# Two transformer blocks on one core: block 1's softmax is divided after its attention matmul, and GpSimd does block 0's clamped normalising

## What is computed

```
x  = x + attn0(ln(x)) + experts0(ln(x))     # block 0
x  = x + attn1(ln(x)) + ffn1(ln(x))         # block 1

attn0: 16 heads of 16 channels, causal, scores + slope * (k - q)
       attn = maximum(softmax(scores), 1e-10);  attended = attn @ v;  attended @ out_w.T + out_b
attn1: 16 heads of 16 channels, causal
       y = softmax(q @ k.T * scale) @ v;  y @ Wo + bo
```

## Time and profile before

| | us |
|---|---|
| median of 3 runs (lowest, highest) | 873.58 (872.56, 874.31) |
| span of the profiled execution | 874.1 |
| PE busy, DVE busy, ACT busy, POOL busy in it | 689.0, 676.7, 589.6, 179.4 |
| one steady pass (430.8 to 524.5) | 93.7 |
| first pass and setup (0 to 147) | 147 |
| last pass (712.5 to 819.8), final stage (819.8 to 874.1) | 107.3, 54.3 |

### The profile page before, as it was taken

The page is one execution under the profiler, slowest core; times in us unless marked ns, Lnnn a source line. Parts: engine busy times, 40 slices in busy tenths (PEclk is TensorE's granted clock), DMA queues, the critical chain, the costliest instruction groups (busy, mean ns, idle before and its releaser), DMA issues.

```text
span 874.1 us, 19430 instructions
## 1 busy us (share of the span) xinstructions
PE 689.0 (79%) x5824; PEld 538.0 (62%) x5824; DVE 676.7 (77%) x2591; ACT 589.6 (67%) x1753; POOL 179.4 (21%) x205
## 2 busy tenths in 40 slices
PE   0676645889869996989788987899789968897756
PEld 0454434667647775767676775677577756685523
DVE  3978755879877996798688987799679986897485
ACT  2455421787759784888488775978497838966764
POOL 6011021132112212131113211321113111320221
PEclk9889876999989998999989998999899998898965
DMA  6752005040323114030504041312312050300651
GB/s 195 257 144 85 1 1 156 1 145 15 107 64 102 43 57 126 24 121 12 170 1 144 13 132 39 109 36 85 98 66 79 13 156 2 128 18 1 198 187 49
DMA packets 55196, 73.95 MB, mean 85 GB/s; under 512 B 4544, under 2 KB 47680, under 8 KB 55104
## 3 DMA queue, kind: packets, MB, share of 16 engines
q1 hardware_dynamic: 52064, 69.22, 25.9%
q0 software_dynamic: 1056, 2.62, 1.0%
q10 hardware_dynamic: 1984, 1.21, 0.4%
HBM read 42.10 MB, written 30.93 MB: 84 GB/s over the span
## 4 chain that ended last, share of the span: by engine, by line
DVE 31%; PE 26%; issue 18%; ACT 16%; DMA 5%; ACTq 1%; SPq 1%; DVEq 1%; POOL 1%; POOLq 0%
DVE probs L1291 7%; DVE probs L1303 7%; PE gen_ps L948 6%; ACT probs L852 4%; PE gen_ps L991 3%; PE gen_ps L959 3%; PE value_ps L1032 3%; PE gen_ps L979 3%; ACT hid L839 3%; DVE acc L1251 2%; DVE gated L1236 2%; ACT pt L861 2%; PE turn_ps L1009 2%; PE gen_ps L934 1%; DMA gu_lo<-x_dram 1%
## 5 line engine op out<-in xcount | busy, mean ns | idle before, releaser
L852 ACT ACTIVATE probs<-probs,nmax 128x256 f32<-128x256 f32 (+1 forms) x512 | 227.5, 447 | 84.9 <-DVE nmax L1291 84.1
L1291 DVE CUSTOM_DVE_ANT_0 probs<-score_ps,bias 128x256 f32<-128x256 f32 (+1 forms) x512 | 159.9, 350 | 49.5 <-PE score_ps L1003 46.9
L1303 DVE TENSOR_SCALAR probs<-probs,rsum 128x256 f32<-128x256 f32 (+1 forms) x512 | 180.4, 394 | 9.1
L724 POOL TENSOR_TENSOR h_lo<-hid,h_hi 128x512 f16<-128x512 f32 x64 | 76.6, 1197 | 424.5 <-ACT h_hi L832 409.4
L861 ACT ACTIVATE pt<-turn_ps 128x384 f32<-128x384 f32 x256 | 122.1, 477 | 33.2 <-PE turn_ps L1011 33.2
L948 PE MATMUL gen_ps<-xe_hi,gu_hi 128*128 128x256 f16 x512 | 104.4, 288 | 4.6 <-DVE v_sb L1162 4.1
L1009 PE MATMUL turn_ps<-ident,probs 128*128 128x128 f32 x256 | 78.1, 305 | 34.0 <-DVE probs L1303 29.1
L948 PE MATMUL gen_ps<-xe_lo,gu_hi 128*128 128x256 f16 x512 | 104.1, 287 | 0.0
L948 PE MATMUL gen_ps<-xe_hi,gu_lo 128*128 128x256 f16 x512 | 103.4, 286 | 0.0
L852 ACT ACTIVATION_READ_ACCUMULATOR probs<-probs,nmax 128x1 f32 x512 | 97.4, 190 | 0.0
L1002 PE MATMUL score_ps<-k_stack,q_stack 96*128 96x256 bf16 x256 | 73.7, 292 | 24.3 <-DMA k_stack<-scr_k 16.0
(11 more groups left out here) (164 smaller groups left out, 1511.4 us busy)
## 6 DMA issues: line engine op xcount, KB each, us to landing
q_stack<-scr_q SPq DMA_DIRECT2D x32, 384.0 KB, 3.8
k_stack<-scr_k SPq DMA_DIRECT2D x32, 384.0 KB, 5.2
scr_q<-parts SPq DMA_DIRECT2D x16, 384.0 KB, 2.6
scr_k<-parts SPq DMA_DIRECT2D x16, 384.0 KB, 3.3
scr_q<-parts SPq DMA_DIRECT2D x16, 256.0 KB, 3.6
scr_k<-parts SPq DMA_DIRECT2D x16, 256.0 KB, 3.6
x<-in_x SPq DMA_DIRECT2D x8, 256.0 KB, 3.6
scr_q<-parts SPq DMA_DIRECT2D x16, 128.0 KB, 2.9
```

Source lines behind the costliest of these rows:

```text
L724: pool.tensor_tensor(h0_lo[:, e], hid0[:, e], h0_hi[:, e], ALU.subtract).then_inc(s_h0l, 1)
L852: last = act.activation(probs[:, k, lo:hi], probs[:, k, lo:hi], ACT.Exp, scale=-1.0, bias=nmax[:, k, j:j + 1], accum_out=esum[:, k, j:j + 1])
L1291: last = dve.tensor_tensor_reduce(out=probs[:, k, lo:hi], in0=g[:, lo:hi], in1=bias[:, blo:S], scale=-1.0, scalar=BIG, op0=ALU.add, op1=AL ...
L1303: last = dve.tensor_scalar(probs[:, k, lo:hi], probs[:, k, lo:hi], rsum[:, k, j:j + 1], *clamp)
```

## The change

Block 1: the exponentials stay as they are. PE's `turn` waits for the exponential itself (`s_ex`) in place of `s_nm`. ACT puts the row sums in `esum1`, ordered by unit. After each unit DVE takes one reciprocal of them, spread over 16 channels ([128 x 256], L1342 of the new file). PE transposes that in two fp32 matmuls into the free half of the `value_ps` bank (L1071), ACT copies it to `rows1` in place of copying the values, and DVE multiplies values and `rows1` into `at` (L1350).

Block 0: DVE still takes the reciprocal of each head. The two multiply-and-clamp instructions move to POOL's queue (L756), at the place of `norm` in the list.

```
+                if name == "norm" and head_block(st) == 0:          # POOL's queue
+                    k = st.arg % PROBS
+                    wait(pool, s_rz, clamped_before(st, 1))
+                    if st.kind == "steady":
+                        settle(pool, s_gps)
+                    for lo, hi, j in ((0, S, 0), (S, S + P, 1)):
+                        last = pool.tensor_scalar(probs[:, k, lo:hi], probs[:, k, lo:hi], rsum[:, k, j:j + 1], CLAMP,
+                                                  ALU.mult, ALU.max)
+                    last.then_inc(s_nm, 1)
...
+                if name == "value" and st.arg % 2 == 1 and set_block(st) == 1:   # ACT's queue
+
+                    wait(act, s_pv, sets_before(st, 1))
+                    act.activation(rows1[:].rearrange("p t q -> p (t q)"), value_ps[:, S:2 * S], ACT.Copy).then_inc(s_rw, 1)
...
-                    wait(pe, s_nm, heads_before(st, 1))
+                    wait(pe, *((s_nm, clamped_before(st, 1)) if head_block(st) == 0 else (s_ex, heads_before(st, 1))))
...
+                    if l == 1 and r == 1:                            # PE's queue, end of a unit
+
+                        wait(pe, s_rr, unit_of_set(st))
+                        for t in range(NT):
+                            last = pe.transpose(value_ps[:, S + P * t:S + P * t + P],
+                                                rsum1[:, t].rearrange("p h c -> p (h c)"), ident[:])
...
-                if name == "norm":                                   # DVE's queue
-                    s, l = st.arg, head_block(st)
+                if name == "norm" and head_block(st) == 0:
+                    s = st.arg
                     k = s % PROBS
                     wait(dve, s_ex, heads_before(st, 1))
                     dve.reciprocal(rsum[:, k], esum[:, k]).then_inc(s_rz, 1)
-                    wait(dve, s_rz, heads_before(st, 1))
-                    for lo, hi, j in ((0, S, 0), (S, S + P, 1)):
-                        clamp = (CLAMP, ALU.mult, ALU.max) if l == 0 else (None, ALU.mult)
-                        last = dve.tensor_scalar(probs[:, k, lo:hi], probs[:, k, lo:hi], rsum[:, k, j:j + 1], *clamp)
-                    last.then_inc(s_nm, 1)
+                if name == "norm" and head_block(st) == 1 and st.arg % 8 == 7:
+                    wait(dve, s_ex, heads_before(st, 1))
+                    wait(dve, s_pv, st.it.at(2 * H // G4, (st.arg - 7) // G4 - H // G4))
+                    dve.reciprocal(rsum1[:].rearrange("p t h c -> p (t h) c"),
+                                   esum1[:, st.arg % H // 8].rearrange("p t h -> p (t h)").unsqueeze(2)
+                                   .broadcast_to([P, NT * H // 2, C])).then_inc(s_rr, 1)
+                if name == "value" and st.arg % 2 == 1 and set_block(st) == 1:
+                    g = st.arg // 2 % NK
+                    if g == 0:
+                        wait(dve, s_x2, ahead(batch_of(st, 1)).at(NT))
+                    wait(dve, s_rw, unit_of_set(st))
+                    dve.tensor_tensor(at[1][:, g], value_ps[:, 0:S], rows1[:].rearrange("p t q -> p (t q)"), ALU.mult)\
+                       .then_inc(s_at, 1)
...
-    nc = bacc.Bacc("TRN2", target_bir_lowering=False, num_devices=1)
+    nc = bacc.Bacc("TRN2", target_bir_lowering=False, num_devices=1, dynamic_dma_scratch_size=8192)
```

More of the change, by code:

```diff
@@ L264, in sets_before, with clamped_before, units_before, unit_of_set @@
     return st.it.at(2 * H // G4, st.arg - H // G4 + extra)
+def clamped_before(st, extra=0):
+    return st.it.at(H, st.arg % H + extra)
+def units_before(st, extra=0):
+    return batch_of(st, 1).at(2, st.arg % H // 8 + extra)
+def unit_of_set(st):
+    return batch_of(st, 1).at(2, st.arg // 2 % NK + 1)
 def at_before(st):
@@ L371, in two_blocks @@
         rsum = sb("rsum", [P, PROBS, 2])
+        esum1 = sb("esum1", [P, 2, NT, H // 2])
+        rsum1 = sb("rsum1", [P, NT, H // 2, C])
+        rows1 = sb("rows1", [P, NT, P])
         pt = sb("pt", [P, 1 + 3 * TURNED, P])
@@ L489, in two_blocks @@
         s_nm = sem("s_nm")
+        s_rr = sem("s_rr")
+        s_rw = sem("s_rw")
         s_tn = sem("s_tn")
@@ L851, in do @@
                     for lo, hi, j in ((0, S, 0), (S, S + P, 1)):
+                        row = 2 * (s % G4) + s // G4 % 2
+                        total = esum[:, k, j:j + 1] if head_block(st) == 0 else \
+                            esum1[:, s % H // 8, 1 - j, row:row + 1]
                         last = act.activation(probs[:, k, lo:hi], probs[:, k, lo:hi], ACT.Exp, scale=-1.0,
-                                              bias=nmax[:, k, j:j + 1], accum_out=esum[:, k, j:j + 1])
+                                              bias=nmax[:, k, j:j + 1], accum_out=total)
                     last.then_inc(s_ex, 1)
@@ L862, in do @@
                                    ACT.Copy).then_inc(s_ev, 1)
-                if name == "value" and st.arg % 2 == 1:
-                    l = set_block(st)
+                if name == "value" and st.arg % 2 == 1 and set_block(st) == 1:
+                    wait(act, s_pv, sets_before(st, 1))
+                    act.activation(rows1[:].rearrange("p t q -> p (t q)"), value_ps[:, S:2 * S], ACT.Copy).then_inc(s_rw, 1)
+                if name == "value" and st.arg % 2 == 1 and set_block(st) == 0:
                     g = st.arg // 2 % NK
@@ L867, in do @@
                     if g == 0:
-                        nb = batch_of(st, l)
-                        wait(act, *((s_acc, nb.at(NT * ACC_STEPS)) if l == 0 else (s_x2, ahead(nb).at(NT))))
-                    act.activation(at[l][:, g], value_ps[:, 0:S], ACT.Copy).then_inc(s_at, 1)
+                        wait(act, s_acc, st.it.at(NT * ACC_STEPS))
+                    act.activation(at[0][:, g], value_ps[:, 0:S], ACT.Copy).then_inc(s_at, 1)
                 if name == "quant":
```

## The result

The changed kernel takes 926.28 us (median of 4 runs, 925.86 to 928.74), the kernel before 873.94 in the same comparison: a ratio of 1.0634, 95% interval 1.0581 to 1.0687. I had said 864, with a range to 880. The sign is wrong and the time lies outside the range.

The account below looks back on a forecast made before the run. No engine bounds the whole; DVE ends waits in two stretches and alone bounds the final stage. -7.2 - 2.5 + 0 + 3.5 - 3.5 = -9.7 from 874.1 gives 864.4, said as 864, range 850 to 880.

Parts of the forecast that it names:

- The price of POOL's pair: Block 0's multiply-and-clamp pair on POOL: 0.9 us a head, bounds 0.74 and 1.2, from copy, select and two-input rows.
- POOL's queue: Block 0's heads in a steady pass: -1.0 before 453.3, +1.0 between 462 and 476, together 0 in each of 7 passes.
- My own chain of four pieces and four pairs: POOL from 466.05 in a steady pass: 4.8 + 3.6 us, ending at 474.45 for 473.48 before.
- My slower rival: Block 0's pairs behind pieces waiting for ACT, 462 to 476, and first-pass switches; pair about 1.2 us: 882, chance 0.20.
- The first pass: Head turns held behind POOL's switches around two reductions, part coming back on DVE: +3.5 us, bounds -2 and +8.
- the second reduction: First pass, at 101.92: head 30's pair behind it, the layer norm's transposes behind that head's turn: 1 us more.
- The terms of block 1: Gains from DVE's relief: six steady passes at -1.2 us, last pass with its end -2.5, final stage -3.5.
- The rival by which DVE was holding much more: PE's idle time outside the layer norm's and ACT's stretch shrinks, seven passes at -3 us: 848, chance 0.15.
- The reciprocal: Block 1's wide reciprocal on DVE, per unit: 0.42 us, at most 0.85, hidden behind the last head's turn and copy.
- The final stage: DVE alone bounds it; losing 18 L1303 instructions gives -4.2, `at` at the end +0.7: -3.5 us.
- The descriptor area: Halved area could stall POOL's 18 transfers, but the copy behind is needed some 7 us later: costed at nothing.
- DVE's small router instructions stretch: Sign of being wrong: these DVE instructions stretching much against POOL.

Follow-up runs that it names:

- b1_alone: The changed kernel with block 0's clamped pair back on DVE, block 1's part and the smaller descriptor area kept: 860.38 us, 0.989 of the kernel before.

## Why the prediction was wrong, step by step

**The price of POOL's pair: the step that failed first.** "It reads one tensor but does two operations; I take 0.9", between 0.74 and 1.2. It is 1.83 with nothing in its way and 1.93 in the mean. I took the number of tensors read for what sets the price and so the copy and the select as nearest rows; the form sets it. The upper bound was wrong too: the two-tensor rows are a cheaper form, not a dearer one. From 0.97 to 1.83 the ratio goes from 1.0088 to 1.0634, some 48 of the 62 us between forecast and result.

**POOL's queue: undercounted.** I let four pairs in a row count and called the middles' balance 0. With a pair of 0.97 they lose 1.6 us a pass against b1_alone (0.5 against the kernel before). My own chain of four pieces and four pairs, with 1.83 for a pair, would end at 478.2 in place of 473.5: 4.7 us, or 33 in seven passes, where the change loses 57.6 against b1_alone. At the real price POOL runs from 495.38 to 514.86 without a gap, seven pairs and six pieces. My slower rival was the mechanism that happened, at the place that it named, but I gave its pair 1.2 us at most and so 882.

**The clock: left out.** Behind PE's new waits its stretches at 0.50 of the clock are longer; in the middle shown PE is busy 2.6 us more than in b1_alone.

**The first pass: right place, wrong size.** +3.5, bounds -2 and +8; measured +14.4. The turn that I put at 83 came like this:

```profile
84.20 0.47 PE L1042 MATMUL turn_ps<-ident,probs 128*128 128x128 f32 x1 [12.93 <-POOL probs L756]
...
117.06 0.59 PE L992 MATMUL gen_ps<-wd_hi,h_hi 128*128 128x256 f16 x2 [7.40 <-DVE gated L1275]
127.96 0.48 PE L1042 MATMUL turn_ps<-ident,probs 128*128 128x128 f32 x1 [5.62 <-POOL probs L756]
```

The first row is the one wait that I expected. It starts 12.4 us after the 71.81 of before; I had 7 of that on PE's path and some 4 of it coming back. The row sum that the second reduction needs shows what did not come back: DVE ends it at 107.36 for 98.66, 8.7 us late. The other two rows are the second reduction, which I priced at 1. POOL begins its switch at 109.05, behind the pair that ends there, where it had begun at 96.1, ahead of the row sum. So its result starts at 115.33 for 101.92, 13.4 us late, and DVE waits 8.40 us for it where it had waited 3.69: 4.7 more. The last 1 of the 14.4 is left for the last turn. On the way, four pairs in a row take 11.72 us for 7.3 (4 x 1.83), and the next one 3.86. DVE's long instructions of the weights' preparation run beside them:

```profile
91.23 11.72 POOL L756 TENSOR_SCALAR probs<-probs,rsum 128x256 f32<-128x256 f32 x8 [2.34 <-DVE rsum L1338]
...
91.05 2.33 DVE L1133 SCALAR_TENSOR_TENSOR t_sb<-hid,t_delta,t_sb 128x2048 f16<-128x2048 f32 x1
...
95.07 2.27 DVE L1136 CUSTOM_DVE_ANT_0 hid<-hid,t_sb 128x2048 f32<-128x2048 f32 x1
...
104.74 2.62 DVE L1140 CUSTOM_DVE_ANT_0 hid<-t_sb 128x2048 f32<-128x2048 f16 x1
...
115.77 0.15 DVE L1144 TENSOR_SCALAR t_tot<-t_tot 128x1 f32<-128x1 f32 x1 [8.40 <-POOL t_tot L778]
```

**The terms of block 1: right in sum, in part by luck.** -7.2, -2.5 and -3.5 made -13.2; b1_alone gives -1.1%, 9.6 us, with an interval from 5 to 14. But I had them in block 1's heads and the end of the pass, the turns, which gave 0.8 a pass and not 1.2; the six steady middles, which I had at nothing, gave 1.0 each. The last pass up to its layer norm, -2.5, came as -2.1. The rival by which DVE was holding much more, 3 us a pass, did not show: with block 1's part the turns gave back 0.7 to 1.5 a pass. The product at 0.42 was right. **The reciprocal** was not: 1.75 us, for 0.42 and at most 0.85. It hid, as the step said, so that the error cost little: making it short brought perhaps 0.3%. The Trainium skill (VectorE: DVE Perf Modes, Walkthrough: the 8-slice pipeline in each mode) says that the reciprocal runs an iterative divide with a repeat count of 8; the trace agrees that it is far dearer than a product of the same shape, 1.75 to 0.42 us.

**The final stage**, -3.5, came as -4.1 in the changed kernel and between -0.7 and -4.8 in the other kernels with block 1's part, which differ there by little but scatter: not wrong, and not shown closer. **The descriptor area** at nothing: right.

**The signs.** "DVE's small router instructions stretch" was not needed: those with `r_s<-r_s` as scalar products took 7.1 us in all, for 5.3. DVE was busy for 541.1 us, for the 490 that I gave as a sign; 21 of the 51 are the wide reciprocals (28.0 for 6.7), the rest I have not taken apart.

## What to carry to other kernels

Before you move work to an idle engine, find the price of that very form of instruction on it; a row of another form is no bound. An engine's busy share says little about a queue in which the moved work stands between pieces that wait for others: count what stands in a row there, at a price that was measured. Of two changes packed into one, try each alone: here the good one (0.986 to 0.989) was hidden under the bad one (1.079).

## What the runs showed that I had not expected

- On GpSimd the product with a scalar is dearer than the product with a whole tensor: 0.93 against 0.61 us at 128x256, and 0.61 against 0.40 at 128x128. The Trainium skill (GPSIMD Engine Reference, Engine selection) says that GpSimd is about 2x slower than VectorE with two inputs and roughly at line rate with one. Here the order is the other way round. The clamped pair, with one tensor read, takes 1.83 us on GpSimd and 0.55 on VectorE, each with nothing in its way; the product of two tensors of 128x256 takes 0.61 and 0.42 (VectorE's is L1350, with one input in PSUM). The measurement decides.
- GpSimd's pairs stretch beside long VectorE instructions: four took 11.72 us in the first pass, beside two of 2.3 us on 128x2048 and one of 1.2 on 128x1024, where they take 7.3 alone. VectorE's pairs stretch beside GpSimd's: 0.99 for 0.77.
- A microsecond more for each of the 128 pairs costs some 55 us of whole time here (47.7 us from 0.97 to 1.83), and PE's busy time for the same matmuls rises with it: 683.6, 694.3 and 701.3 us at pairs of 0.97, 1.50 and 1.83.
